# A graph layer on one core: z_out rows added by the gathers themselves, z gathers over 128 partitions

## What is computed

```python
in_deg  = minimum(segment_sum(ones, dst), 511)
out_deg = minimum(segment_sum(ones, src), 511)
edge_proj = edge_attr @ W_sum + b_sum
sum3d = segment_sum(edge_proj, src)
cent_term = sigmoid(centralities @ W_cent + b_cent)
vor_term  = sigmoid(voronoi_values @ W_vor + b_vor)
h = relu(layernorm(x))
return x + h + z_in[in_deg] + z_out[out_deg] + cent_term + vor_term + sum3d
```

## Time and profile before

| | |
|---|---|
| median of 3 runs | 3028.99 us |
| lowest, highest run | 3013.37, 3032.68 us |
| span of the profiled execution | 3079.2 us |
| PE busy | 1621.7 us (53%) |
| DVE busy | 1683.0 us (55%) |
| ACT busy | 819.8 us (27%) |
| POOL busy | 1853.9 us (60%) |
| DMA moved | 451.89 MB, mean 147 GB/s |

### The profile page before, as it was taken

One profiled execution on the slowest core, in us unless ns is written; L12 is line 12 of the kernel. 1 busy time (PEld: TensorE's weight loads), 2 busy tenths in 40 slices (PEclk: granted clock), 3 DMA queues, 4 the chain that ended last, 5 costly groups with the idle time before them and its releaser, 6 DMA issues.

```text
span 3079.2 us, 40112 instructions
## 1 busy us (share of the span) xinstructions
PE 1621.7 (53%) x8689; PEld 1230.9 (40%) x8689; DVE 1683.0 (55%) x5737; ACT 819.8 (27%) x4073; POOL 1853.9 (60%) x1869
## 2 busy tenths in 40 slices
PE   5644555455555432226555554444456665568766
PEld 1223444344333320014444444333355554456655
DVE  7554456666666631346656654333455554468866
ACT  3312222232322332442232322222222222200323
POOL 5556665556565667665555655656655555556676
PEclk7756666666666655557767777767777777789988
DMA  4245433334444443334555555555556666579896
GB/s 122 85 127 151 116 106 107 99 104 122 122 121 121 126 135 106 88 107 137 155 152 164 160 160 161 143 151 148 155 156 181 183 187 178 169 189 231 210 248 187
DMA packets 485070, 451.89 MB, mean 147 GB/s; under 512 B 72407, under 2 KB 444637, under 8 KB 484828
## 3 DMA queue, kind: packets, MB, share of 16 engines
q1 hardware_dynamic: 402782, 300.08, 37.0%
q0 software_dynamic: 78752, 136.44, 14.1%
q10 hardware_dynamic: 3294, 12.80, 1.3%
HBM read 319.28 MB, written 129.59 MB: 146 GB/s over the span
## 4 chain that ended last, share of the span: by engine, by line
another core or an unknown queue 34%; DVE 19%; PE 17%; issue 15%; ACT 7%; DMA 3%; SPq 2%; POOL 2%; DVEq 1%; ACTq 0%; POOLq 0%
PE bank L1001 8%; ACT junk L864 6%; DVE hot_dh L605 3%; DVE hot_n L670 3%; DVE acc L697 2%; DVE hot_dl L605 2%; PE bank L949 2%; POOL sorted L513 2%; DMA edge_ring<-in_L_gnn_z_out_dram,out_i 2%; SPq L408 2%; DVE gate_normed L736 2%; PE bank L984 1%; PE bank L1026 1%; DVE hot_t L605 1%
## 5 line engine op out<-in xcount | busy, mean ns | idle before, releaser
L513 POOL DMA_INDIRECT sorted<-edge_ring,pos_i x1660 | 1605.8, 967 | 1103.1 <-DVE pos_i L799 633.4
L1001 PE MATMUL bank<-piece_ring,hot_n 128*125 128x129 f32 x4920 | 885.4, 336 | 260.0 <-DVE hot_n L670 209.0
L864 ACT ACTIVATE junk<-bank,mark_col 128x100 bf16<-128x100 f32 x1664 | 550.4, 343 | 1748.6 <-remote 1221.3
L1001 PEld LDWEIGHTS bank<-piece_ring,hot_n 128*125 128x125 f32 x4920 | 823.2, 241 | 367.0 <-DVE hot_n L670 248.7
L697 DVE TENSOR_TENSOR acc<-bank,acc 125x129 f32 x1230 | 352.8, 287 | 698.6 <-remote 523.9
L984 PE MATMUL bank<-hot_w,after_b 128*128 128x400 bf16 x416 | 189.3, 455 | 806.1 <-ACT junk L864 560.7
L670 DVE SCALAR_TENSOR_TENSOR hot_n<-bank,wkey,piece_ring 128x250 f32<-128x250 f32 x1230 | 579.9, 472 | 11.8 <-issue 5.2
L984 PEld LDWEIGHTS bank<-hot_w,after_b 128*128 128x128 bf16 x416 | 49.5, 119 | 866.8 <-ACT junk L864 594.3
L864 ACT ACTIVATION_READ_ACCUMULATOR junk<-bank,mark_col 128x1 f32 x1664 | 338.1, 203 | 12.3 <-issue 12.3
L605 DVE TENSOR_TENSOR hot_dl<-dst_parts,bank 128x400 bf16<-128x400 bf16 x416 | 148.0, 356 | 337.1 <-remote 305.5
L1026 PE MATMUL bank<-hot_dl,hot_dh 128*125 128x100 bf16 x1661 | 207.2, 276 | 237.4 <-DVE hot_dh L605 197.6
(11 more groups left out here) (109 smaller groups left out, 1183.2 us busy)
## 6 DMA issues: line engine op xcount, KB each, us to landing
piece_ring<-sorted SPq DMA_DIRECT2D x1230, 130.0 KB
edge_ring<-in_edge_attr_dram SPq DMA_DIRECT2D x332, 320.0 KB
sorted<-edge_ring,pos_i POOLq DMA_INDIRECT x1660
base<-in_x_dram SPq DMA_DIRECT2D x20, 560.0 KB
out_dram<-base ACTq DMA_DIRECT2D x19, 560.0 KB
out_dram<-base SPq DMA_DIRECT2D x9, 560.0 KB
base<-out_dram SPq DMA_DIRECT2D x9, 560.0 KB
edge_ring<-in_L_gnn_z_out_dram,out_i POOLq DMA_INDIRECT x100
```

What stands on the lines that cost most here:

```text
L513: g.indirect_dma_start(rows, bass.IndirectOffsetOnAxis(index, 0), edge_ring[:, slot, at, :], None).then_inc(s_scatter[slot], 16)
L864: last = a.activation(junk[:, t, :], part[:, t // 2, :, t % 2], ACT.Relu, bias=mark_col[:, :], accum_out=pos_f[:, q % 4, t:t + 1])
L1001: last = t_.matmul(to, hot_n[:, n % HOT_SLOTS, k, :], piece_ring[:, n % PIECE_SLOTS, k, 0:SUM], start=(k == 0), stop=(k == ROW_GROUPS[s] - 1))
```

## The change

The z_out rows have no slots any more. POOL issues each z_out gather after the product add of the window, with an add as the DMA's operation and the row in base as its destination. The 100 z_out adds of DVE go, and the stores of ACT wait for the landings of the gathers of their windows (s_onto). All z gathers, z_in too, now cover 128 partitions. So that the three more partitions hold defined data, deg_i and out_i are set to 0 once and one load fills partitions 125 to 127 of base. The rings shrink from 15 to 5 and from 18 to 9 slots.

```diff
-GATHERS = 15
-GUEST_GATHERS = 18
+GATHERS = 5
+GUEST_GATHERS = 9
...
-                       + [(ahead + ADD_LAG + w, "product", w) for w in range(NW)]
-                       + [(ahead + Z_LAG + w, "z_out", w) for w in range(NW)])
+                       + [(ahead + ADD_LAG + w, "product", w) for w in range(NW)])
...
-    others = [(kind, w) for _, kind, w in tail_adds if kind == "z_out" or kind == "z_in" and w < ROW_SLOTS]
+    others = [(kind, w) for _, kind, w in tail_adds if kind == "z_in" and w < ROW_SLOTS]
+    onto = [("z_out", w) for w in range(NW)]
...
-    z_order = sorted(guests + others, key=lambda g: (step_of[g] - lead.get(g, 0), g[0] == "z_out"))
+    step_of.update({("z_out", w): ahead + Z_LAG + w for w in range(NW)})
+    z_order = sorted(guests + others + onto, key=lambda g: (step_of[g] - lead.get(g, 0), g[0] == "z_out"))
...
                 if q == x_quad[0]:
                     sp.wait_ge(s_keys, KEYS)
+                    sp.dma_start(base[NODE_P:P, :, :].rearrange("p a b -> p (a b)"),
+                                 x[0:(P - NODE_P) * ROW_SLOTS, :].rearrange("(p a) d -> p (a d)", a=ROW_SLOTS)).then_inc(s_spare, 16)
...
+            pool.wait_ge(s_spare, 16)
             for kind, w in z_order:
+                if kind == "z_out":
+                    pool.wait_ge(s_out_deg, w // COUNTED + 1)
+                    pool.wait_ge(s_added, added["product", w])
+                    g.indirect_dma_start(base[:, w % ROW_SLOTS, :], None, z_out[:, :],
+                                         bass.IndirectOffsetOnAxis(out_i[:, w:w + 1], 0),
+                                         compute_op=ALU.add).then_inc(s_onto[store_of(w)], 16)
+                    continue
...
-                g.indirect_dma_start(places[n % len(places)][0:NODE_P, :], None, table[:, :],
-                                     bass.IndirectOffsetOnAxis(index[0:NODE_P, w:w + 1], 0)
+                g.indirect_dma_start(places[n % len(places)][:, :], None, table[:, :],
+                                     bass.IndirectOffsetOnAxis(index[:, w:w + 1], 0)
                                      ).then_inc(landed[n % len(places)], 16)
...
+            v.memset(deg_i[:, :], 0)
+            v.memset(out_i[:, :], 0)
...
-                act.wait_ge(s_added, max(added["z_out", w] for w in range(w0, w1)))
+                act.wait_ge(s_onto[i], 16 * (w1 - w0))
```

## The result

The changed kernel takes 3064.11 us (median of 4 runs, 3058.41 to 3068.82), the kernel before 3027.9 us (median of 4 runs, 3013.37 to 3032.68). The ratio is 1.0124, 95% interval 1.0096 to 1.0152: slower by 36 us. The forecast was 3024 us, within 1%.

What follows compares the result with a forecast made beforehand. It took POOL as limit of the middle windows, with DMA nearly level. Terms -2 (stage 1), -2.7 (stage 2), -3 (stage 3) and +2.5 (end) gave -5.2 us, hence 3024 us; range 3002 to 3062, chance 0.50.

Steps and rivals of the forecast that it cites:

- What bounds before: Kernel before, last part: POOL limits the middle windows at 121.8 of 127.0 us, with DMA engines nearly level at 1.01.
- Part 1: z gathers over 128 partitions: POOL period falls from 1.505 to 1.27 us, plain and accumulating alike; accumulating upper bound 2.23 us.
- a rival of 0.06: Accumulating gather costs POOL 2.23 us, slowing all windows of the last part: +64 us, 3093 us; chance 0.06.
- stage 2: Middle 54 windows of the last part, 127.0 us before, POOL the limit; forecast 2.7 us shorter.
- stage 3: Last 27 windows of the last part, 49.4 us before, no full resource; forecast 3 us shorter.
- Part 2: 100 z_out adds leave DVE, 33 us in all: worth 5 us in the first 19 and last 27 windows, nothing between.
- stage 1: First 19 windows of the last part, 36.2 us before, no full resource; forecast 2 us shorter.
- Part 3: POOL's queue with fewer slots: 89 instead of 80 gathers in the middle windows, 113.0 us of POOL instead of 127.0.
- Part 4: DMA time in the middle windows: at 72.3 ns per accumulated row 124.3 us, so the 14.0 us gain shrinks to 2.7.
- The third rival: The accumulate costs DMA twice, 144.6 ns per row, middle windows 155.2 us: +29 us, 3058 us; chance 0.20.
- Part 5: New waits: stores waiting for landings cost nothing with 15 us of slack, except after the last product add, 2.5 us lost.
- The end: Last product add to end of span: about 7.5 instead of 5.1 us, 2.5 us lost.

Runs made afterwards that it cites:

- b2: The kernel before, unchanged, traced again on a chip of the faster kind: 2484.1 us.
- e1_plain128: The kernel before with its z gathers on 128 partitions and index lists cleared, z_out still added by DVE: 0.9827 of before on a faster chip.
- e2: The changed kernel with z_out gathers that overwrite instead of adding: 0.9901 of before on a faster chip.
- e13: The changed kernel with its 9 first guest gathers issued one behind every third row gather instead of in one run: 1.01 of before on a faster chip.
- e9: The changed kernel with 18 guest slots instead of 9: 1.012 of before on a slower chip.
- e6: The kernel before with plain 128-partition z gathers and 9 guest slots instead of 18: 1.0158 of before on a slower chip.
- e7: The same kernel as e1_plain128 (kernel before, plain 128-partition z gathers), run on a slower chip: 1.0092 of before.
- e4_iota: The changed kernel with overwriting z_out gathers and an iota of 0.55 us on POOL ahead of each: 1.0085 of before on a slower chip.
- e8: The same kernel as e2 (changed kernel, overwriting z_out gathers), run on a slower chip: 1.0084 of before.

## Why the prediction was wrong, step by step

- **What bounds before: not refuted.** On kind B the plain gathers alone shortened the products from 203.3 to 176 to 179 us, but they relieve POOL and the DMA engines at once, so no run tells which of the two limits it was. On kind A the same gathers shortened nothing (211.9 and 215.6 us).
- **Part 1, plain gathers at 0.97 us: right** (0.95 to 1.0 us). Landings became shorter as hoped: on one chip the median fell from 7.6 us (b2) to 4.4 us (e1_plain128). That agrees with the rule cited there from the Trainium skill, DMA: Bandwidth & Descriptors, section "Why a DMA increments its semaphore by 16 and not by 1".
- **Part 1, "for the accumulating form I take the same 1.27 us": this is the step that failed.** It is 1.85 us. The bound of 2.23 us was in the text, but as a rival of 0.06. With 1.85 us the forecast's own counts give stage 2 as 54 x 1.85 + 35 x 1.27 = 144 us (measured 137.2, since POOL lets z_out gathers slip into stage 3), and 100 x 0.58 = 58 us more POOL work over the whole; the 48 us between e2 and e13 fit that. I had set the price by scatters, which move as many rows but don't add; nothing in the trace of before added in a DMA, and the middle of the two bounds, 1.75 us, would have been close, by luck.
- **Part 2 (-5 us in stages 1 and 3): void.** With POOL as limit of all stages, DVE's 33 us are worth nothing; stage 1 went from 36.2 to 36.0, stage 3 from 49.4 to 59.6 us.
- **Part 3, fewer slots: harmless in the changed kernel**, where 18 slots bring nothing (e9); in the old order 9 slots alone go with 23 us more of product time (e6 against e7, two chips).
- **Part 4, DMA time: not the limit.** q0 took 43.1% of 16 x 137.2 us = 946 us. With 33 plain gathers at 48 ns per row, the 51 x 128 accumulated rows have (946 - 203)/6528 = 114 ns each, an estimate, against 72.3 taken. e2_no_add has 31.6% of 16 x 104.2 us for 10.66 MB, about 50 ns per KB, so by this estimate, which holds queueing too, the add doubles a row's time. That agrees in direction with the two reads per write that the forecast cited from the Trainium skill, Collectives: The Full Stack, section "The bandwidth ceiling: the fold count and why AG ≠ RS ≠ AR". But DMA share was 0.93, because the other queues took 1080 us and not 1294, and e4_iota without the second read still runs at POOL's pace. The third rival's time was near (3058 us) for a reason that wasn't the cause: that is luck.
- **Part 5, stores and end: wrong in what waits.** A landing alone fits into the 15 us ahead of a store; POOL's lag doesn't, and ACT waited 69.8 us. The end was put at +2.5 and is +10.1 us, since three gathers are still owed when the last product stands. The end is longer without the add too (11.4 and 11.6 us in e8 and e2 against 5 us), so a part of that was mis-sized by itself.
- **What no step had:** on kind A, plain 128-partition gathers cost 0.9% instead of gaining 1.7%, with remote waits and gaps between folds. Eleven profiles and the pair e4 and e8, on different chips, go with POOL's pace. That the pace is the cause was not shown by a controlled pair on one chip. Why DVE's folds start late there stays open, as does the difference of 540 us between the kinds, nearly all in the scatter part. It bears on the forecast: e8_no_add, with no add to pay for, is still 0.84% over before on kind A. So the kernel would have been slower there than forecast even at the plain price.

So on kind B the add's price is the larger part: without it the changed kernel gains 1.0%, with it it loses 1.0%, and the plain gathers alone gain 1.7%. On kind A, where the result was measured, the price makes POOL the limit at 231 of 233 us. There it mostly takes the place of another loss, of open cause, that the change would otherwise have had.

## What to carry to other kernels

Here an add in an indirect DMA moved work from VectorE to GpSimd: 0.33 us of a DVE that had time became 0.6 us on a POOL that had none. Before trading one for the other, price the new form on its own engine with a few instances, and if that engine is the limit, don't take the kindest row for a form that the trace has never shown. A change worth 1% should be run on more than one chip: the best kernel on one kind (plain 128-partition gathers) is 1.7% faster there and 0.9% slower on the other.

## What the hardware showed that I had not expected

- The accumulating gather of 128 rows costs POOL 1.55 us against 0.95 us plain, and 2.01 us at 125 rows; a plain one of 125 rows 1.20 to 1.23 us.
- Between the last scatter and the first product, the queue of POOL with gathers of 128 rows of 1 KB had 3377 packets for 9.13 MB, that with gathers of 125 rows 8896 packets for 8.99 MB.
- The same kernel takes 2,484 us on some chips and 3,020 to 3,081 us on others, with the waits called remote on the second kind alone.
- On that kind, the product loop with a slower stream of indirect DMAs (e4_iota, 212.7 us) was 17 us shorter than with an unhindered one (e8_no_add, 229.9 us), in one profile each on two chips.
